# A GNN kernel: scatters spread over three stages, and one-hot tiles with another layout

## What is computed

```python
edge_index = jnp.stack([src, dst])
h = relu(_layernorm(x)); x = x + L0(h, ...)        # attention over relations, edges grouped by src
h = relu(_layernorm(x))                            # L1: three graph attention layers, 4 heads
for i in range(3):
    xs, xd = h @ Ws[i], h @ Wd[i]
    e = leaky_relu(alpha_s[src] + alpha_d[dst], 0.2)
    h = segment_sum(xs[src] * seg_softmax(e, dst), dst) + bias[i]
x = x + h
h = relu(_layernorm(x)); x = x + L2(h, src, dst)   # graph convolution, normalised by degrees
h = relu(_layernorm(x)); x = x + L3(h, src, dst, edge_type)   # attention, edges grouped by dst
```

## Time and profile before

| | us |
|---|---|
| median of 3 runs | 10835.07 (10820.09 to 10841.47) |
| the profiled execution | 10830.81 |
| its span in the profile | 10829.0 |
| DVE busy | 7986.2 (74%) |
| POOL busy | 6921.5 (64%) |
| PE busy | 6746.9 (62%) |
| ACT busy | 5754.5 (53%) |

### The profile page before, as it was taken

How to read it: one execution, slowest core, us unless ns; L and a number is a source line. 1 busy time by engine, 2 the same in 40 slices (tenths; PEclk the granted TensorE clock), 3 DMA queues, 4 the chain that set the end, 5 groups by cost and what they waited for, 6 DMA issues and landing times. The chain is left out here.

```text
span 10829.0 us, 223526 instructions
## 1 busy us (share of the span) xinstructions
PE 6746.9 (62%) x64938; PEld 5475.7 (51%) x64939; DVE 7986.2 (74%) x22059; ACT 5754.5 (53%) x12392; POOL 6921.5 (64%) x5770
## 2 busy tenths in 40 slices
PE   3984952236666566656666467676676668466665
PEld 2973952235554454545555355455554544366665
DVE  9779778847777677767777678778787870477776
ACT  4224222236666566646666477767777760155554
POOL 0777731057776777767777488868868710466665
PEclk8555555568887788778888798889898889777777
DMA  0111114322223223223222211111111126322222
GB/s 22 57 37 28 60 36 144 124 62 53 52 53 48 49 53 53 52 45 52 53 53 53 39 49 43 49 43 45 49 37 49 49 86 249 73 48 46 46 45 44
DMA packets 420007, 630.47 MB, mean 58 GB/s; under 512 B 273511, under 2 KB 330305, under 8 KB 396201
## 3 DMA queue, kind: packets, MB, share of 16 engines
q0 software_dynamic: 192432, 385.10, 17.0%
q1 hardware_dynamic: 160080, 158.87, 4.7%
q10 hardware_dynamic: 67401, 85.32, 2.2%
HBM read 527.43 MB, written 103.02 MB: 58 GB/s over the span
## 5 line engine op out<-in xcount | busy, mean ns | idle before, releaser
L895 POOL DMA_INDIRECT l_land<-table,l_words x3744 | 3596.3, 961 | 1342.5 <-issue 1158.6
L1682 POOL DMA_INDIRECT ell<-gat_stage_pay,gat_stage_at x816 | 1929.5, 2365 | 248.6 <-issue 248.6
L1365 PE MATMUL left_product_ps<-k_w,messageT 128*128 128x128 f32 x5616 | 1045.5, 343 | 530.2 <-ACT messageT L1400 530.2
L1365 PEld LDWEIGHTS left_product_ps<-k_w,messageT 128*128 128x128 f32 x5616 | 881.4, 239 | 736.6 <-ACT messageT L1400 736.6
L2231 PE MATMUL rel_ps<-relation_parts,hot 128*128 128x128 bf16 x11328 | 831.1, 248 | 414.8 <-DVE hot L2330 414.8
L1779 ACT COPY gat_probT<-gat_ps 128x512 f32<-128x512 f32 (+1 forms) x2100 | 1026.5, 550 | 112.8 <-PE gat_ps L1722 100.1
L2231 PEld LDWEIGHTS rel_ps<-relation_parts,hot 128*128 128x128 bf16 x11328 | 810.7, 114 | 436.2 <-DVE hot L2330 436.2
L244 POOL DMA_INDIRECT ell<-pay,position x816 | 842.4, 1032 | 289.3 <-issue 280.0
L1359 PE MATMUL left_turned_ps<-ident,message 128*128 128x128 f32 x2808 | 560.2, 334 | 725.4 <-DVE message L1491 725.4
L1722 PE MATMUL gat_ps<-ident,gat_logit 128*128 128x128 f32 x3750 | 629.7, 307 | 605.1 <-ACT gat_logit L1771 589.7
L1416 ACT ACTIVATE weighed<-kept,l_prob 128x128 f32 x2784 | 888.9, 391 | 59.1 <-ACT l_prob L961 59.0
(11 more groups left out here) (332 smaller groups left out, 15741.2 us busy)
## 6 DMA issues: line engine op xcount, KB each, us to landing
gcn_edges<-counts SPq DMA_DIRECT2D x50, 1600.0 KB, 8.1
l_land<-table,l_words POOLq DMA_INDIRECT x3744
rows<-low_dram SPq DMA_DIRECT2D x34, 1536.0 KB
counts<-pair_turned_sb ACTq DMA_DIRECT2D x12, 3200.0 KB, 9.4
logs<-pair_logs ACTq DMA_DIRECT2D x12, 3200.0 KB, 18.2
ell<-pay,position POOLq DMA_INDIRECT x816
ell<-gat_stage_pay,gat_stage_at POOLq DMA_INDIRECT x816
l_words<-ell SPq DMA_DIRECT2D x476, 8.0 KB
```

What stands on the lines that cost most here:

```text
L895: pool.indirect_dma_start(self.land[:, p, s, :], None, table[:, :], bass.IndirectOffsetOnAxis(ap=self.words[:, p, s, 0:1], axis=0)).then_i ...
L1365: mm = pe.matmul(right_ps[:, k * H + j, :], messageT[:, k, j, :], k_w[:, :], start=True, stop=True)
L1682: pool.indirect_dma_start(c.ells[1][:, :], bass.IndirectOffsetOnAxis(ap=stage_at[n % 2][:, t:t + 1], axis=0), stage_pay[n % 2][:, t, :], N ...
```

## The change

Two things are changed.

The second sort's 816 scatters are dealt out anew: 144 (`EARLY_TILES`) at the start of GpSimd's work in `count_pairs`, 96 (`LATE_TILES`) in `graph_convolution` between the scatter and the gather of rows, and the other 576 in `graph_attention`, in 72 parts of 8. Their places and contents come by two DMAs of SP for each group. GpSimd's clearing of `counts` goes.

In `count_pairs` the one-hot tiles have another layout, `hi_hot` [block, source node] and `lo_hot` [destination, source node], and are compared with iotas spread out once at the start, so that the innermost dimension of every operand has a step of one element. The matmuls read them with steps of 16 and 128 elements. Where a pair is in its first group of edges (`g < 1`), ACT copies the products to `counts`, with destinations innermost in what it writes, and the vector engine only makes one-hot tiles; further groups are still added by the vector engine. The pair's matmuls now stand ahead of the earlier pair's transposes on TensorE, and the same holds for copies on ACT.

```diff
@@ -987,14 +987,16 @@
+EARLY_TILES, LATE_TILES = 144, 96
@@ -1013,9 +1015,11 @@
-        hi_hot = sb("pair_hi_hot", [P, P, NB], BF16)
-        lo_hot = sb("pair_lo_hot", [P, 2, CHUNK, P], BF16)
+        hi_hot = sb("pair_hi_hot", [P, NB, P], BF16)
+        lo_hot = sb("pair_lo_hot", [P, 2, P, CHUNK], BF16)
+        hi_iota, lo_iota = sb("pair_hi_iota", [P, NB, P], BF16), sb("pair_lo_iota", [P, P, CHUNK], BF16)
...
+        early_at, early_pay = sb("early_at", [P, EARLY_TILES], I32), sb("early_pay", [P, EARLY_TILES, 2], I32)
@@ -1048,6 +1052,8 @@
             def _(sp):
+                sp.dma_start(early_at[:, :], c.position_dram[:, 0:EARLY_TILES]).then_inc(early_in, 16)
+                sp.dma_start(early_pay[:, :, :], a["payloads"][1][:, 0:EARLY_TILES, :]).then_inc(early_in, 16)
                 sp.wait_ge(plan_ready, 1)
@@ -1068,18 +1074,19 @@
             @block.gpsimd
             def _(pool):
-                for p in range(PAIRS):
-                    if p >= 2:
-                        pool.wait_ge(turned, (p - 1) * 2 * TURNS)
-                        pool.wait_ge(logged, p - 1)
-                    nc.gpsimd.memset(counts[p % 2][:, :, :, :], 0.0).then_inc(cleared, 1)
+                pool.wait_ge(early_in, 32)
+                for t in range(EARLY_TILES):
+                    pool.indirect_dma_start(c.ells[1][:, :], bass.IndirectOffsetOnAxis(ap=early_at[:, t:t + 1], axis=0),
+                                            early_pay[:, t, :], None).then_inc(early_placed, 16)
+                pool.wait_ge(early_placed, 16 * EARLY_TILES)
...
             @block.tensor
             def _(pe):
                 pe.wait_ge(plan_ready, 1)
 
                 def turn_counts(p, k, parts):
-                    pe.wait_ge(summed, p + 1)
+                    many, first = steps(pe, p)
+                    pe.wait_ge(kept, (first + many) * CHUNKS_OF + 2)
@@ -1104,17 +1111,20 @@
                             for j in range(CHUNK):
                                 for b in range(2):
                                     half = slice(b * GROUP, (b + 1) * GROUP)
-                                    mm = pe.matmul(chunk_ps[u % 2][:, b, j * NB:(j + 1) * NB], lo_hot[half, u % 2, j, :],
-                                                   hi_hot[half, u * CHUNK + j, :], start=True, stop=True)
+                                    mm = pe.matmul(chunk_ps[u % 2][:, b, j * NB:(j + 1) * NB], lo_hot[half, u % 2, :, j],
+                                                   hi_hot[half, :, u * CHUNK + j], start=True, stop=True)
                             mm.then_inc(counted, 1)
-                    turn_counts(p, k, parts)
-
-                pair(0, 0)
+
+                pair(0)
                 with pe.Fori(0, PAIRS // 2 - 1) as two:
                     for k in range(2):
-                        pair(two * 2 + (k + 1), 1 - k)
-                pair(PAIRS - 2, 1)
-                pair(PAIRS - 1, 0, 1)
+                        pair(two * 2 + (k + 1))
...
+                pair(PAIRS - 2)
+                turn_counts(PAIRS - 3, 0, 2)
+                pair(PAIRS - 1)
+                turn_counts(PAIRS - 2, 1, 2)
+                turn_counts(PAIRS - 1, 0, 1)
@@ -1123,12 +1133,20 @@
-                def pair(p, k, earlier, parts=2):
+                def pair(p, k):
                     many, first = steps(act, p)
                     with act.Fori(0, many) as g:
                         n = act.snap(first + g)
                         act.wait_ge(split_turned, n + 1)
                         nc.scalar.copy(splitT[:, :, :], split_ps[:, :, :]).then_inc(split_moved, 1)
+                        with act.If(g < 1):
+                            for u in range(CHUNKS_OF):
+                                act.wait_ge(counted, n * CHUNKS_OF + (u + 1))
+                                nc.scalar.copy(counts[k][:, :, :, u * CHUNK:(u + 1) * CHUNK].rearrange("p h b j -> p b h j"),
+                                               chunk_ps[u % 2][:, :, 0:CHUNK * NB]
+                                               .rearrange("p b (j h) -> p b h j", h=NB)).then_inc(kept, 1)
+
+                def finish(p, k, earlier, parts=2):
@@ -1151,14 +1169,18 @@
-                pair(0, 0, 0)
+                pair(0, 0)
+                pair(1, 1)
+                finish(0, 0, 0)
                 with act.Fori(0, PAIRS // 2 - 1) as two:
                     for k in range(2):
-                        pair(two * 2 + (k + 1), 1 - k, two + k)
+                        pair(two * 2 + (k + 2), k)
+                        finish(two * 2 + (k + 1), 1 - k, two + k)
                         tell(two * 2 + k, k)
-                pair(PAIRS - 2, 1, PAIRS // 2 - 1)
...
+                pair(PAIRS - 1, 0)
+                finish(PAIRS - 2, 1, PAIRS // 2 - 1)
                 tell(PAIRS - 3, 0)
-                pair(PAIRS - 1, 0, PAIRS // 2, 1)
+                finish(PAIRS - 1, 0, PAIRS // 2, 1)
                 tell(PAIRS - 2, 1)
@@ -1192,14 +1214,13 @@
-                for k in range(2):
-                    V.memset(logs[k][:, :, :, :], 0.0)
+                V.tensor_copy(hi_iota[:, :, :], spread(c.iota_rb[:, 0:NB], [P, NB, P], 2))
+                V.tensor_copy(lo_iota[:, :, :], spread(c.iota_rb[:, :], [P, P, CHUNK], 2))
...
                 def pair(p, k):
                     many, first = steps(v, p)
                     V.tensor_copy(left[:, :], degree[:, bass.ds(p * 2, 2)])
                     v.drain()
-                    stand(v, turns, cleared, p + 1)
@@ -1217,25 +1238,28 @@
                         v.wait_ge(split_moved, n + 1)
-                        V.tensor_tensor(hi_hot[:, :, :], spread(c.iota_rb[:, 0:NB], [P, P, NB], 1),
-                                        spread(splitT[:, 1, :], [P, P, NB], 2), ALU.is_equal)
+                        V.tensor_tensor(hi_hot[:, :, :], hi_iota[:, :, :], spread(splitT[:, 1, :], [P, NB, P], 1),
+                                        ALU.is_equal)
 
                         def hot(u):
-                            V.tensor_tensor(lo_hot[:, u % 2, :, :], spread(c.iota_rb[:, :], [P, CHUNK, P], 1),
-                                            spread(splitT[:, 0, u * CHUNK:(u + 1) * CHUNK], [P, CHUNK, P], 2),
+                            V.tensor_tensor(lo_hot[:, u % 2, :, :], lo_iota[:, :, :],
+                                            spread(splitT[:, 0, u * CHUNK:(u + 1) * CHUNK], [P, P, CHUNK], 1),
                                             ALU.is_equal).then_inc(hot_ready, 1)
 
                         hot(0)
                         hot(1)
-                        for u in range(CHUNKS_OF):
-                            v.wait_ge(counted, n * CHUNKS_OF + (u + 1))
-                            total = counts[k][:, :, :, u * CHUNK:(u + 1) * CHUNK].rearrange("p h b j -> p b j h")
-                            V.tensor_tensor(total, chunk_ps[u % 2][:, :, 0:CHUNK * NB]
-                                            .rearrange("p b (j h) -> p b j h", h=NB), total, ALU.add).then_inc(kept, 1)
-                            if u + 2 < CHUNKS_OF:
-                                hot(u + 2)
-                        v.drain()
-                    v.sem_inc(summed, 1)
+                        with v.If(g < 1):
+                            for u in range(2, CHUNKS_OF):
+                                v.wait_ge(counted, n * CHUNKS_OF + (u - 1))
+                                hot(u)
+                        with v.If(g > 0):
+                            for u in range(CHUNKS_OF):
+                                v.wait_ge(counted, n * CHUNKS_OF + (u + 1))
+                                total = counts[k][:, :, :, u * CHUNK:(u + 1) * CHUNK].rearrange("p h b j -> p b h j")
+                                V.tensor_tensor(total, chunk_ps[u % 2][:, :, 0:CHUNK * NB]
+                                                .rearrange("p b (j h) -> p b h j", h=NB), total, ALU.add).then_inc(kept, 1)
+                                if u + 2 < CHUNKS_OF:
+                                    hot(u + 2)
@@ -1244,11 +1268,14 @@
                 pair(0, 0)
-                with v.Fori(0, PAIRS // 2) as two:
+                pair(1, 1)
+                with v.Fori(0, PAIRS // 2 - 1) as two:
                     for k in range(2):
-                        pair(two * 2 + (k + 1), 1 - k)
+                        pair(two * 2 + (k + 2), k)
                         tell(two * 2 + k, k)
-                tell(PAIRS - 1, 0)
+                pair(PAIRS - 1, 0)
+                for p in range(PAIRS - 3, PAIRS):
+                    tell(p, p % 2)
@@ -1593,9 +1620,9 @@
-    PART = 12
-    PARTS = z.tiles // PART
-    assert PARTS * PART == z.tiles and PARTS <= LAYERS * NB
+    PART = 8
+    PARTS = (z.tiles - EARLY_TILES - LATE_TILES) // PART
+    assert PARTS * PART + EARLY_TILES + LATE_TILES == z.tiles and PARTS <= LAYERS * NB
@@ -1654,7 +1681,7 @@
-                    part = slice(n * PART, (n + 1) * PART)
```

(9 more changed lines are left out.)

13 lines of the change are left out of this document (9 added, 4 removed).

## The result

The changed kernel takes 10443.1 us (median of 4 runs, 10437.7 to 10457.3), the one before 10835.2 (10820.1 to 10841.5): ratio 0.964, interval 0.9628 to 0.9652. The forecast was 10248 (10190 to 10325). The profiled execution took 10442.8 us (span 10441.0). The sum made ahead came to 10243.9, so 198.9 us are missing.

| landmark | before | after | gained | forecast |
|---|---|---|---|---|
| end of the counts stage (first gather of the next) | 2202.49 | 2034.30 | 168.2 | 278.9 |
| from there to attention's first large operation | 3951.3 | 3958.9 | -7.6 | 0 |
| attention, first to last of these operations | 2676.6 | 2354.9 | 321.7 | 311 |
| from there to the convolution's first scatter | 52.1 | 51.7 | 0.4 | 0 |
| convolution, first half (that scatter to its row gathers) | 200.9 | 299.2 | -98.3 | -3 |

The account below looks back on a forecast made before the run. Counts was taken as a chain of three engines taking turns, attention as vector engine plus waits for gathers, convolution as full TensorE. 10830.8 - 311 - 278.9 + 3 = 10243.9, plus 4.3 for the median: 10248 us (10190 to 10325).

Parts of the forecast that it names:

- Attention, from 13 requests to 9: Attention stage: fewer GpSimd requests an item cut waits for gathers from 401 to 90 us, gain 311 (266 to 336).
- One-hot tiles: Counts stage, vector engine: unit-step 2-byte operands halve the element part, tiles of 3.49 and 2.30 us become 1.82 and 1.23.
- rival A: Counts stage: one-hot tiles keep the full price, as a broadcast operand may not count as unit step; 10364 us, chance 0.10.
- Sums become copies, chunk pace 1.30: Counts stage: slowest of tile (1.14), products (0.6 to 1.2) and ACT copy (0.9 to 1.7) sets a chunk, 1.30 us.
- B: Rival, counts stage: copies or products set the pace, at 1.9 us a chunk; 10310 us, chance 0.13.
- D: Rival, counts stage: strided weight load can't run beside the product, so slower than before; 11049 us, chance 0.03.
- A pair in 30.95 us: Counts stage: the new chain of a pair takes 30.95 us against 51.09, for 11 pairs 221 us gained.
- First cast at 1507.1: Counts stage's start: clears and delayed small operations go, two spread iotas (about 3 us) come; 28.5 us become 12.3.
- End of the stage: Counts stage: last cast at 1865.4, stage ends at 1923.6, 278.9 us earlier.
- The 144 early scatters lie beside this. Cost 0: Counts stage: about 14 scatters a pair fit, through after some ten pairs, near 1800, at no cost.
- Rival C: Counts stage: tiles lock GpSimd out, early scatters at 3.6 us each end it 95 us later; 10343 us, chance 0.04.
- I take 3 us, 0 to 12: Convolution: the 96 late scatters' small writes raise the DMA share of 0.65 beside a full TensorE, costing 3 us.

Follow-up runs that it names:

- e4: As e1, but lo_hot laid out as before, its tile made from a broadcast with innermost step zero: 13374.2 us, single run.
- v3: Changed kernel with 66 early scatters, 6 a pair one at a time, none in the convolution, 33 in each attention layer's first two items: 10332.4 us, ratio 0.9541.
- e1: Changed kernel without any moved scatter, all 816 in attention, 12 an item: 13314.4 us, ratio to before 0.9787.
- c2: Changed kernel with the 96 late scatters moved into attention and 96 gathers of 32 rows in their place in the convolution: 10333.7 us, single run.
- a1: The changed kernel again, unaltered, on another chip: 10411.7 us, ratio to before 0.9614.
- e2: Changed kernel with the 96 late scatters moved from the convolution into attention, 16 more in each layer's first two items: 13239.7 us, ratio to before 0.9725.
- v1: Changed kernel with 132 early scatters one at a time, none in the convolution, 684 in attention, 50 of them in its last item: 10349.3 us, ratio 0.9552.

## Why the prediction was wrong, step by step

- *Attention, from 13 requests to 9*: right. Waits of 80.2 us against 90, gain 321.7 against 311.
- *One-hot tiles*: right, 1.83 and 1.22; rival A falls. e4 shows that the innermost step of zero had kept the old price.
- *Sums become copies, chunk pace 1.30*: right, 1.26, with some luck: 1.30 was picked from a range without knowing which term sets it. It was the products, at 1.18 the top of 0.6 to 1.2; the copy took 0.83, below the range taken and half of the 1.6 feared, with steps in what it reads. So B and D fall.
- *A pair in 30.95 us*: right, 30.7 to 31.3 in full periods wherever no scatters run (the last period 32.5 to 32.8).
- *First cast at 1507.1*: 1514.1. The first spread alone takes 3.48 us and the second 1.22, not 3 together, and the groups' ids were there 11 us behind their issue, beside scatters. In v3, where no scatter runs yet, it was 3 us, and the first cast comes at 1505.7.
- *End of the stage*: 8 us more than counted, 7.6 of them the wait for a store of two pairs earlier (e1).
- *"The 144 early scatters lie beside this. Cost 0"*: the step that failed. They were issued by 1748 (forecast: near 1800), and cost 95.8 us on the way. Only GpSimd's time was weighed, not what its rows do to the stores that the shorter stage issues every 31 us. Rival C had nearly the right sum, 95, for a reason that the trace refutes: a scatter came every 1.7 us and not every 3.6, and nothing waited for the last one.
- *"I take 3 us, 0 to 12" for the convolution*: failed, 98.3. The 0.65 of the earlier trace rows is a mean over both halves; the first half alone was at 0.81 and 272 GB/s, and from TensorE's first product there to its last at 0.94 and 318 GB/s. TensorE was called full; it was busy 318 of 407 us, and already waited 12.8 us for a block of edges. What was missing beside these shares is that a scattered write takes far more of the engines than its bytes: c2 added as many small packets there, all of them reads, and paid nothing.

The missing 198.9 us: 95.4 between the casts, 7.0 before the first, 8.3 at the end, 95.3 in the convolution, 7.6 between counts and attention that no run explains (2.4 in a1), less 10.7 from attention and some 4 elsewhere. The mechanisms of the gain were right; the price of where the scatters went was left out. That the scatters caused both prices is shown, by taking them out (e1, e2, v1 to v3). How much of it is stretched packets and how much the stops called "issue" and "remote" is shown for the convolution on kind A, where there are no such stops, and stays open for counts.

## What to carry to other kernels

An engine that is idle is no free place for its work: ask of every small DMA which large transfers run beside it and whether it writes, and read the DMA share of that stretch alone. Here scatters were free at a share of 0.35; at 0.62 six a pair were nearly free and eleven were not; at 0.81 all of them paid 0.7 to 1.1 us each. A queue's own row doesn't show what it costs the others; compare the time per packet of the large one with and without it. When one half of a change shortens a stage, cost the other half against the new, shorter stage: 144 scatters were free in 680 us and cost 83 to 96 in 424.
